# Re-ordered set-up and small paced mask pieces in a two-layer graph kernel, with the last unit rows transposed inside the first block

## What is computed

```python
def _L0_gnn_ref(x, adj, beta):
    norm2 = jnp.linalg.norm(x, axis=1, keepdims=True)
    cos = beta[0] * (x @ x.T) / (norm2 @ norm2.T + 1e-07)
    masked = cos + (1.0 - adj) * -1000000000.0
    P = jax.nn.softmax(masked, axis=1)
    return P @ x

def _L1_gnn_ref(x, edge_index, weight):
    support = jnp.matmul(x, weight)
    return jnp.matmul(edge_index, support)

x = _layernorm(x + _L0_gnn_ref(x, adj, L0_gnn_beta), axis=-1)
x = _layernorm(x + _L1_gnn_ref(x, adj, L1_gnn_weight), axis=-1)
```

## Time and profile before

| | us |
|---|---|
| median of 3 runs | 489.86 |
| lowest, highest | 489.72, 491.61 |
| the profiled execution, its own time | 491.9 |
| its span in the profile | 490.1 |
| PE busy | 466.5 (95%) |
| DVE busy | 376.5 (77%) |
| ACT busy | 319.5 (65%) |
| GpSimd busy | 52.7 (11%) |

### The profile page before, as it was taken

How to read it: one execution, slowest core, us unless ns; L and a number is a source line. 1 busy time by engine, 2 the same in 40 slices (tenths; PEclk the granted TensorE clock), 3 DMA queues, 4 the chain that set the end, 5 groups by cost and what they waited for, 6 DMA issues and landing times.

```text
span 490.1 us, 8879 instructions
## 1 busy us (share of the span) xinstructions
PE 466.5 (95%) x3491; PEld 303.6 (62%) x3491; DVE 376.5 (77%) x623; ACT 319.5 (65%) x374; POOL 52.7 (11%) x65
## 2 busy tenths in 40 slices
PE   0988999999999999999999999999989999999994
PEld 0555667667666767677676676676664455555484
DVE  4978999999999999999999999999963022211253
ACT  5887988898898889889888988987961000000000
POOL 5310010210020120111102002000100000000011
PEclk9998999999999999999999999999999999999998
DMA  8989999999999999999998997960052010011111
GB/s 193 109 93 123 124 114 132 121 152 167 107 152 111 154 149 117 158 139 80 141 125 119 150 121 123 92 143 22 0 173 86 1 43 23 22 44 43 44 43 44
DMA packets 102250, 50.20 MB, mean 102 GB/s; under 512 B 70448, under 2 KB 98768, under 8 KB 102224
## 3 DMA queue, kind: packets, MB, share of 16 engines
q0 software_dynamic: 18480, 16.78, 41.7%
q1 hardware_dynamic: 83456, 33.06, 32.1%
q10 hardware_dynamic: 288, 0.07, 0.1%
HBM read 77.40 MB, written 22.82 MB: 204 GB/s over the span
## 4 chain that ended last, share of the span: by engine, by line
PE 83%; DMA 8%; DVE 3%; issue 2%; ACT 1%; POOL 1%; POOLq 0%; DVEq 0%; ACTq 0%
PE psum L976 22%; PE psum L913 20%; PE psum L917 11%; PE psum L892 10%; PE psum L890 10%; PE psum L891 10%; DMA adjT<-adj_bytes 4%; DMA adj_bytes<-in_adj 3%; PE psum L986 1%; DVE E L667 1%; DVE el L675 1%; DMA adjT<-in_x 1%; POOL rn L384 1%; ACT eh L462 1%; ACT E L453 1%
## 5 line engine op out<-in xcount | busy, mean ns | idle before, releaser
L913 PE MATMUL psum<-xaug,eh 128*128 128x257 f16 x1024 | 185.0, 274 | 3.9 <-DVE el L675 3.7
L453 ACT ACTIVATE E<-psum,sc 128x1024 f32<-128x1024 f32 x128 | 154.3, 1206 | 38.3 <-PE psum L892 37.3
L917 PE MATMUL psum<-xaug,el 128*128 128x129 f16 x1024 | 176.0, 221 | 0.0
L667 DVE SCALAR_TENSOR_TENSOR E<-E,adjT 128x1024 f32<-128x1024 f32 x128 | 155.8, 1217 | 12.6 <-ACT E L453 6.4
L675 DVE SCALAR_TENSOR_TENSOR el<-E,eh 128x1024 f16<-128x1024 f32 x128 | 155.6, 1216 | 0.0
L462 ACT ACTIVATE eh<-E 128x1024 f16<-128x1024 f32 x128 | 134.4, 1050 | 7.2 <-DVE E L667 6.8
L913 PEld LDWEIGHTS psum<-xaug,eh 128*128 128x128 f16 x1024 | 99.5, 98 | 30.3 <-DVE el L675 6.2
L976 PE MATMUL psum<-adjT,uT 128*128 128x512 fp8e4 (+1 forms) x576 | 112.1, 355 | 0.0
L917 PEld LDWEIGHTS psum<-xaug,el 128*128 128x128 f16 x1024 | 100.5, 98 | 14.0 <-issue 0.3
L890 PE MATMUL psum<-uT 128*128 (+1 forms) x256 | 98.4, 384 | 1.1 <-ACT E L453 1.1
L891 PE MATMUL psum<-uT 128*128 (+1 forms) x256 | 98.3, 384 | 0.0
(11 more groups left out here) (73 smaller groups left out, 159.6 us busy)
## 6 DMA issues: line engine op xcount, KB each, us to landing
adj_bytes<-in_adj POOLq DMA_DIRECT2D x31, 512.0 KB, 11.9
adjT<-in_x SPq DMA_DIRECT2D x4, 512.0 KB, 6.9
xres<-in_x SPq DMA_DIRECT2D x8, 256.0 KB, 3.3
q_row<-norms SPq DMA_DIRECT2D x8, 256.0 KB, 8.2
x_rows<-x SPq DMA_DIRECT2D x8, 256.0 KB, 2.8
E<-x_rows SPq DMA_DIRECT2D x8, 256.0 KB, 2.9
out<-E SPq DMA_DIRECT2D x16, 128.0 KB, 2.2
x_parts<-x1p SPq DMA_DIRECT2D x7, 256.0 KB, 3.6
```

The costliest lines, as they stand in the source:

```text
L453: nc.scalar.activation(E[:, m % RING, :, :], S[m % 2], ACT.Exp, bias=col(C_BB), scale=col(C_BS)).then_inc(e_done, 1)
L667: nc.vector.scalar_tensor_tensor(out=e, in0=e, scalar=EPRE, in1=mask_bytes(b, m), op0=ALU.mult, op1=ALU.min).then_inc(masked, 1)
L913: return nc.tensor.matmul(O[t][:, 0:XC], eh[:, s, a, cols], xaug[:, j, :], start=start, stop=stop)
L917: return nc.tensor.matmul(O[t][:, 0:D + 1], el[:, s, a, cols], xaug[:, j, 0:D + 1], start=False, stop=False)
```

## The change

It touches set-up, block 0 and the tail.

- `x`: the first chunk is loaded in two halves, with a semaphore `x_head` for the first; squares of chunk 0 are shared out accordingly.
- `FIRST` now covers all of block 0: two pieces of one pair and seven of two pairs. From the fifth on a cast waits until the piece three before it is in (`first_in[f - 3]`). On GpSimd the powers for the norms stand between the first casts in another order.
- The unit rows of chunk 3 are made by GpSimd (`unit_rows_p`, eight instructions ahead of the fifth cast); those of chunk 2 stay with DVE, but stand behind the low part of pair 2.
- Groups 4 to 7 are no longer transposed through banks 4 to 7 behind the scores of pair 2. Groups 4 and 5 are transposed ahead of the scores of pair 6, into banks 0 and 1, groups 6 and 7 ahead of those of pair 10, into banks 2 and 3: the banks of the scores. Pairs 6 to 9 therefore use the other score area than before (`bank_of`), and the scores of pairs 7 and 11 wait until DVE has read the transposed groups.
- PE turns groups 0 and 1 ahead of the extremes' transposes, and the second of these stands between the halves of pair 0's scores. The steps behind the scale of `xaug` are spread over DVE's list. The store of the norms moves up on SP.
- Statistics use `bn_aggr`, one instruction a row tile, and one small instruction, in place of seven.
- In the last half PE adds the residual rows by a product with the identity into the same bank as the weights' product, and DVE reads PSUM directly.

```diff
-    FIRST = [(0, 1), (1, 1), (2, 1), (3, 1)]
+    FIRST = [(0, 1), (1, 1), (2, 2), (4, 2), (6, 2), (8, 2), (10, 2), (12, 2), (14, 2)]
...
         def u_bank(g):
-            return 4 + g % 4
+
+            return 4 + g if g < 4 else g - 4
...
+        TURN_AT = {6: 4, 10: 6}
+
+        def bank_of(m):
+
+            return (m + 1) % 2 if 6 <= m < 10 else m % 2
...
+                if c == 0:
+                    head = slice(0, CT // 4)
+                    sp.dma_start(rows_in_twos(xfull)[:, head, :], x_c[:, head, :]).then_inc(x_head, 16)
+                    half = slice(CT // 4, CT // 2)
...
-            load_mask(0)
+            for f, (k, n) in enumerate(FIRST):
+                sp.wait_ge(first_cast[f], 16)
+                sp.dma_start_transpose(adjT[:, 0, k:k + n, :],
+                                       first_piece(adj8_v, f).bitcast(U16)).then_inc(first_in[f], 16)
+                if f == 3:
+                    sp.wait_ge(q_moved, 1)
+                    sp.dma_start(q_v, q_T[:, :]).then_inc(q_stored, 16)
             sp.dma_start(rows_in_twos(xres[:, :, :]), x_v[0]).then_inc(xres_in, 16)
-            sp.wait_ge(q_moved, 1)
-            sp.dma_start(q_v, q_T[:, :]).then_inc(q_stored, 16)
...
             def cast_first(f):
+
+                if f > 3:
+                    pool.wait_ge(first_in[f - 3], 16)
                 pool.dma_start(first_piece(adj8_v, f), first_piece(adj_v, f)).then_inc(first_cast[f], 16)
...
+            def unit_rows_p(c):
+                pool.wait_ge(rn_done, c + 1)
+                for t in range(c * CT, (c + 1) * CT):
+                    last = nc.gpsimd.tensor_scalar(work[:, t, :], xfull[:, t, :], rn[:, t:t + 1], USC, ALU.mult, ALU.mult)
+                last.then_inc(u_done_p, 1)
+
             pool.wait_ge(x_in[0], 16)
             cast_first(0)
             inverse_norms(0)
             cast_first(1)
+            inverse_norms(1)
             cast_first(2)
-            inverse_norms(1)
-            cast_first(3)
             inverse_norms(2)
             inverse_norms(3)
-            for k in range(1, 2 * MP + 2):
+            cast_first(3)
+            unit_rows_p(NC - 1)
+            for f in range(4, len(FIRST)):
+                cast_first(f)
+            for k in range(MP, 2 * MP + 2):
                 cast(k)
...
             for m in range(NP):
-                if m == 2:
-                    for g in range(4, UG):
-                        uT_hi_part(g)
+                if m in TURN_AT:
+                    uT_hi_part(TURN_AT[m])
+                    uT_hi_part(TURN_AT[m] + 1)
                 exp_pair(0, m)
...
-            def combine(o, base, n=IT, order=chain):
...
+            def mean_var(o, n=IT, order=chain):
+                for t in range(o, o + n):
+                    last = nc.vector.bn_aggr(mv[:, t, :], stats[:, t, :])
+                last.then_inc(order, 1)
...
-                    if m == 1:
-                        uT_lo_part(3)
                     if m > 0:
                         split_lo(0, m - 1)
                     if m == 1:
-                        for g in range(4, UG):
-                            uT_lo_part(g)
+                        uT_lo_part(3)
+                    if m == 3:
+                        unit_rows(2)
+                    if m + 1 in TURN_AT:
+                        uT_lo_part(TURN_AT[m + 1])
+                        uT_lo_part(TURN_AT[m + 1] + 1)
...
+                if m in TURN_AT:
+
+                    pe.wait_ge(e_done, m - 1)
+                    turn_unit_rows(TURN_AT[m])
+                    turn_unit_rows(TURN_AT[m] + 1)
+
+                    pe.wait_ge(e_done, m)
                 pe.wait_ge(uT_lo, m // 2 + 1)
+                if m - 1 in TURN_AT:
+                    pe.wait_ge(uT_lo, TURN_AT[m - 1] + 2)
...
+            def add_rows(ts):
+
+                pe.wait_ge(x1_in[1], 8 * NB)
+                for t in ts:
+                    nc.tensor.matmul(C_last[t - HT][:, 0:D], ident[:, :], stage[:, 1, t, 0:D], start=True, stop=False)
...
-            weights(r, C_half[1], range(HT, IT), NB + 1)
+            add_rows(range(HT, IT))
+            pe.wait_ge(sum_moved, NB + 1)
+            for t in range(HT, IT):
+                cols = slice(HB + t % 2, BI, 2)
+                last = nc.tensor.matmul(C_last[t - HT][:, 0:D], sumT[:, r % 2, cols], w_sb[:, :],
+                                        start=False, stop=True)
+            last.then_inc(c_done, 1)
```

More of the change, by code:

```diff
@@ L452, in exp_pair @@
                     act.wait_ge(lo_done, n - RING + 1)
-                nc.scalar.activation(E[:, m % RING, :, :], S[m % 2], ACT.Exp,
+                nc.scalar.activation(E[:, m % RING, :, :], S[m % 2 if later(b) else bank_of(m)], ACT.Exp,
                                      bias=col(C_BB), scale=col(C_BS)).then_inc(e_done, 1)
@@ L647, in add_small_term @@
                         dve.wait_ge(fix, base + 4)
-                        s = S[m % 2][:, a, part]
+                        s = S[m % 2 if later(b) else bank_of(m)][:, a, part]
                         done = nc.vector.tensor_tensor(s, s, num, ALU.mult)
@@ L892, in scores @@
                     last = nc.tensor.matmul(o, lj, hi, start=False, stop=True)
+                    if not later(b) and m == 0 and a == 0:
+                        turn_extremes()
                 last.then_inc(s_filled, 1)
```

200 lines of the change are left out of this document (100 added, 100 removed).

## The result

The changed kernel takes 492.29 us in the median of 20 runs (491.30 to 496.41); the kernel before takes 491.25 in runs beside them (fastest 489.29; one of its 20 took 831.11 and, like one of 1747.61 in `e_lofirst` below, counts in no ratio). The ratio is **1.0031, 95% interval 1.0017 to 1.0046**: some 1.5 us slower by the ratio, 1.0 by the difference of the medians, and within 0.5%. The forecast was 490.8 against 489.86, a ratio of 1.002; 489.86 was the median of three runs of the kernel before, where the 20 runs beside the changed kernel gave 491.25.

What follows compares the result with a forecast made beforehand. PE was taken to bound the kernel from 65 us on, and mask transfers, through DVE, to hold it in block 0. Start 0, clock +1.3, early piece +0.3, tail −0.7: +0.9 on 489.86 gives 490.8 us, range 487.4 to 493.4.

Steps and rivals of the forecast that it cites:

- that sum: Block 0, DVE's list from mask of pair 1 to low part of group 5: 16.3 us, seen by PE at 37.25.
- the estimate's low end: Tail statistics: two bn_aggr and one instruction take 0.5 us if one costs 0.16, up to 0.8 if double.

Runs made afterwards that it cites:

- e_lofirst: Changed kernel with DVE's low parts of uT for groups 4 to 7 made one instruction earlier; ratio 0.9998 to the kernel before, median 491.01 us.
- e_turnback: Changed kernel with groups 4 to 7 again turned early through banks 4 to 7, chunk 2 scaled before the first mask; ratio 0.9950 to the kernel before, 488.26 us.
- a_again: Changed kernel, unedited, run as a second draw; ratio 1.0013 to the kernel before, median 491.33 us.
- tb_again: Second draw of `e_turnback`, unedited; ratio 0.9949 to the kernel before, median 488.68 us.

## What to carry to other kernels

Price a removed wait against its size in a typical execution, not in the one profiled: where it is a wait on a transfer it varies, and what replaces it in an engine's program order hardly does. Before two traces are compared, see where each stands among the runs of its own kernel. Before scarce banks are lent to a second user in mid-stream, lay the reader's whole instruction list out up to the hand-back; that sum was right here to 0.4 us. And with the DMA engines near full, read the next block's first wait before booking a gain in this one.

## What the runs showed of the hardware

- **A ring of transfers has two phases.** Casts and transposes that wait for one another run either two and two or one beside the other. SyncE's transposes behind 56 us took 119 us in the one and 266 in the other; in one kernel the phase made no difference (`e_turnback`, whose trace has 247 us, at 0.9950, and 0.9954 with the phase forced), in the other it cost 1.3% (1.0144 against 1.0015 with the phase forced). DVE's waits in blocks 0 and 1 did not tell it: the longest in the slow one was 0.57 us.
- **The half clock came and went for one program.** In after PE idled 1.98 us before 30.74 and the granted clock was 0.72 over 30 to 36 us; in `a_again` it idled 1.54 before 30.53 and the clock stayed at 1.00. In `tb_again` 3.03 us of idle before 70.03 were followed by 0.72 over 70 to 76 us, but in `a_again` 3.23 us before 37.46 by 1.00 from there to 56 us. So the length of one gap did not decide it.
- **Small instructions beside large ones have tails.** A GpSimd scaling of 128×128 took 0.36 us in the median and 1.33 to 3.34 in one or two of eight, and a DVE mask beside them 1.82 in place of 1.21 in one execution, 1.25 to 1.40 in the five others with these scalings.
- **Two `bn_aggr` took 0.25 us** together, less than the 0.16 each of the estimate's low end.
